# Decoder layer kernel: H chunks made earlier and in all quadrants, DVE and POOL kept off a shared port, W2's two parts in one product

## The chip, the cores and the metric

One core of a Trainium2 chip. The metric is the device time of one execution in microseconds, as the median of several runs; a lower time is better. The engines are called PE (TensorE), PEld (its weight loads), DVE (VectorE), ACT (ScalarE), POOL (GpSimd) and SP (SyncE, which here only issues DMAs).

## The reference

A decoder layer on `x` (4 x 512 rows of 256) with a second input of 4 x 64 context rows:

```
x = x + attn(layernorm(x))        # 16 heads of 16; softmax over the 4 rows of axis 0
x = x + xattn(layernorm(x), ctx)  # 16 heads of 64, per batch row of 512 queries, 64 keys
x = x + ffn(layernorm(x))         # 8 experts of 256 -> 1024 -> 256

def ffn(x):
    route_prob = softmax(xf @ Ws + bs).T              # (8, 2048)
    route_vals, routes = top_k(route_prob, 256)       # each expert takes its 256 best rows
    h = gelu(einsum('ekd,edf->ekf', xf[routes], W1) + b1)
    out = (einsum('ekf,efd->ekd', h, W2) + b2) * route_vals[..., None]
    return zeros.at[routes].add(out)
```

All is float32.

## The kernel before

One core does the whole layer. Every engine has one queue, written out by hand, and waits on semaphores. The rows are 16 tiles of 128 (`NT` = 16), four (`NJ`) per batch row; `D` = 256 is two chunks (`MC`) of 128.

**Precision.** A product whose operands are split into two fp32r parts is three matmuls (`product3`, L929 to L931): hi x hi, hi x lo, lo x hi. Other products are fp32 and show two records per matmul.

**Part 1** (to about 80 us) is the first attention, in four blocks of rows `j`, and among its steps the folded weights of the cross attention: `KV_product(c)` makes keys and values of chunk `c` (two of the 16 heads), `G_product(c)` multiplies the keys with the query weights. ACT evicts the high part of G (`G_evac`) and DVE the low part (`low_parts`). `mix_transpose(j)` needs POOL's sum `acc`, which needs DVE's `scale`; `y_product(j)` is followed by DVE's `add_residual(j)` and `statistics2(j)`, and POOL's inverse deviations. `turns` (L245 on) writes out by hand in which order each PSUM bank is used; `bank_free` and `bank_full` wait accordingly.

**Part 2** (to about 221 us) is the cross attention. `H` folds values and output weights: `pe_H` makes chunk `c` for the four batch rows (eight matmuls of 64 x 64 x 256 in two quadrants of the array), `act_H` evicts the high part, `dve_H` subtracts for the low part. The eight chunks are made in pairs ahead of the first four steps (`H_STEPS`, k = -3 to 0) of a software pipeline. A step `k` on PE (`pe_step`) is: the transposes of the probabilities of tile k, the transposes of the normalised rows of tile k+3 (`xn2`), the scores of tile k+2, the output product of tile k, and the logits of tile k-1. DVE (`dve_step`) takes the sums of tile k+1, the low parts of the probabilities (`PT_low`) and of `xT`, then the maximum (L1261) and the shifted scores (L1266) of tile k+2; ACT the exponential (L1097); POOL the division (L1137) and the additions to X. W1 and W2 of experts 0 to 3 are loaded and split (`W_high` on ACT, `W_low` on POOL) in the later steps; the last two halves are in the drain, the last of them after POOL's last normalised rows.

**Part 3** (about 221 to 248 us) finds each expert's 256th probability in 15 rounds (`SEARCHES`): DVE counts two trials (L1416, L1419), ACT one, PE adds over partitions, DVE takes the new floor. POOL meanwhile splits the probabilities into three bf16 parts (L1518 to L1522).

**Part 4** does the experts. For each one a list of its rows is made by DVE's one-hot (`onehot_of`, L1757) and 16 small matmuls (`list_of`, L1593), read by DVE (`read_list`), and used by POOL's indirect DMAs: a gather (L1698) of 256 rows and at the end a scatter-add (L1718). PE transposes the rows, makes the up product (8 x 2 x 3 matmuls of 256 columns) and the down product (2 x 8 x 3). ACT's GELU writes `hbuf`, two slots deep, and DVE makes `h_hi` (L1797) and `h_lo` (L1799); GELU of group n waits for `h_ready` n-1. `outputs(e)` scales and adds the result to `ybuf` (L1738). Ahead of expert 0, PE makes lists 0 and 1, seven unread matmuls (`UNREAD`, L1612), the transposes, and list 2; list 3 stands after the fourth of the up product's eight parts:

```
list_of(FIRST_LISTS[0])
list_of(FIRST_LISTS[1])
for _ in range(UNREAD): ...
transposes(EXPERTS[0])
list_of(FIRST_LISTS[2])
```

DVE reads lists 2 and 3 before it enters the loop over the experts.

Of the kernel before, what the change touches and what calls it, by code (L numbers as in the profile page):

```python
# [13 lines left out]
def build_program(nc, A, out):  # L14
# [11 lines left out]
    P = 128  # L26
# [93 lines left out]
    with ctx:  # L120
# [6 lines left out]
        def overlay(*sets):  # L127
# [5 lines left out]
            for k in order[:-1]:  # L133
# [11 lines left out]
        eps_col, warm = region([("eps_col", [P, 1], F32), ("warm", [P, 1], F32)])  # L145
# [31 lines left out]
        (H_hi, H_lo), attn, (W2_hi, W2_lo), (_, W2_raw) = overlay(  # L177
            [("H_hi", [P, CB, NC, D], F32R), ("H_lo", [P, CB, NC, D], F32R)],
            [("xn1", [P, T, D], F32), ("xnT", [P, MC, T, P], F32), ("q", [P, 2, T, D], F32),
             ("dif0", [P, NP, D], F32), ("sq", [P, NP, D], F32), ("acc", [P, T, D], F32),  # L180
             ("wqa", [P, MC, D], F32), ("dif1", [P, NP, D], F32),
             ("owT", [P, MC, D], F32), ("Nw", [P, MC, D], F32),
             ("MTs", [P, MC, P], F32), ("dist", [P, NP, HS], F32),
             ("Wk", [P, MC, HK], F32), ("bias_raw", [3 * NC, P], F32),
             ("b1_raw", [E * FC, P], F32), 
             ("outb_bc", [P, D], F32), ("Wq", [P, MC, HK], F32)],
            [("W2_hi", [P, 4, FC, D], F32R), ("W2_lo", [P, 4, FC, D], F32R)],
            [("beside2", [P, 4, FC, D], F32), ("W2_raw", [P, 4, FC, D], F32)])
        (xn1, xnT, q, dif0, sq, acc, wqa, dif1, owT, Nw, MTs, dist, Wk,
         bias_raw, b1_raw, outb_bc, Wq) = attn  # L190
# [65 lines left out]
        G_BANKS = (5, 5, 5, 2, 5, 2, 5, 2)  # L256
# [4 lines left out]
        def G_turns(c):  # L261
            return [(f"G{c}{m}", G_BANKS[c] + m, G_ready, MC * c + m + 1) for m in range(MC)]

# [8 lines left out]
        turns += KV_turns(3) + block_turns("M", 2) + G_turns(3) + KV_turns(4) + block_turns("y", 2) + G_turns(4)  # L272
        turns += KV_turns(5) + block_turns("M", 3) + G_turns(5) + KV_turns(6) + block_turns("y", 3)
        turns += KV_turns(7) + G_turns(6) + G_turns(7)
        part1 = len(turns)
        H_BANKS = ((4, 7), (5, 0), (1, 4), (7, 5), (4, 5), (7, 4), (5, 7), (4, 5))
        for c in range(NC):
            turns += [(f"H{c}{m}", H_BANKS[c][m], H_ready, 2 * c + m + 1) for m in range(2)]
# [594 lines left out]
        def sc(slot):  # L873
            return [banks[2 * slot], banks[2 * slot + 1]]
# [993 lines left out]
```

## Time and profile before

| | |
|---|---|
| median of 3 runs | 367.15 us (365.62 to 367.66) |
| the profiled execution | 367.29 us, span 365.5 us |
| PE busy | 321.0 us, 88% |
| DVE, ACT, POOL busy | 286.6, 189.5, 195.7 us |
| mean granted TensorE clock | 0.943 of full speed |

The span runs from the first to the last instruction; the execution's own time has some 1.8 us more. A busy PE is a PE with matmuls in flight: they are pipelined, so the duration of one is longer than the distance to the next. In the rows below times are us from the start of the span, mean durations ns.

### The profile page before, as it was taken

The page shows a single profiled execution, that of the slowest core. Times are in us where ns is not written, and L with a number is a line of the kernel's source. Part 1 is how long each engine was busy: PE and PEld are TensorE (multiplying, and loading weights), DVE is VectorE, ACT ScalarE, POOL GpSimd, SP SyncE. Part 2 cuts the span into 40 slices and gives each one's busy share as a digit, 9 for nine tenths or more (in the row PEclk, how much of TensorE's full clock was granted, in tenths as well). Part 3 has the DMA queues.
Part 4 walks back from the last instruction along what each step waited for, and adds up shares of the span by engine and source line. Part 5 has one row for each costly group of instructions (what it writes and reads, how often), then busy time and mean ns, then how long its engine had stood idle before and what let it go on. Part 6 is the DMA issues. An engine that isn't in the chain of part 4 may idle for free.

```text
span 365.5 us, 6473 instructions
## 1 busy us (share of the span) xinstructions
PE 321.0 (88%) x2350; PEld 290.6 (79%) x2350; DVE 286.6 (78%) x637; ACT 189.5 (52%) x374; POOL 195.7 (54%) x248
## 2 busy tenths in 40 slices
PE   7989998899979999999999991126999999999991
PEld 7877886675559999999999881116999999999991
DVE  3888888858777888888888778778578699689860
ACT  2677655446464457657764643682417546652230
POOL 3778789723042537888788764605224515543222
PEclk9999999999989999999999996555999999999997
DMA  8950000000000135143331537301158757611222
GB/s 251 382 208 1 2 0 2 0 0 3 0 2 0 38 121 165 39 145 97 105 130 57 159 103 230 116 1 43 45 165 240 184 204 190 173 20 40 30 30 29
DMA packets 24047, 34.29 MB, mean 94 GB/s; under 512 B 1784, under 2 KB 20560, under 8 KB 23888
## 3 DMA queue, kind: packets, MB, share of 16 engines
q1 hardware_dynamic: 20112, 29.36, 24.6%
q0 software_dynamic: 3072, 4.20, 6.5%
q10 hardware_dynamic: 832, 0.32, 0.4%
q8 instruction: 19, 0.31, 0.4%
q14 instruction: 12, 0.10, 0.1%
HBM read 27.58 MB, written 6.29 MB: 93 GB/s over the span
## 4 chain that ended last, share of the span: by engine, by line
PE 73%; DVE 13%; POOL 6%; ACT 4%; issue 2%; POOLq 0%; DVEq 0%; ACTq 0%
PE bank L929 13%; PE bank L931 13%; PE bank L930 13%; PE bank L939 4%; PE q_banks L929 4%; PE q_banks L930 4%; PE q_banks L931 4%; DVE flags_all L1419 2%; PE bank L1593 2%; PE bank L778 2%; PE q_banks L723 2%; PE bank L741 2%; PE bank L757 2%; POOL acc L410 1%; PE bank L957 1%
## 5 line engine op out<-in xcount | busy, mean ns | idle before, releaser
L1718 POOL DMA_INDIRECT out_x<-ybuf,idx x16 | 26.0, 1628 | 59.8 <-DVE ybuf L1738 57.7
L1137 POOL TENSOR_TENSOR prob<-prob,rsum 128x1024 f32<-128x1024 f32 x15 | 28.6, 1905 | 17.3 <-DVE rsum L1245 17.3
L929 PE MATMUL bank<-W_hi,h_hi 128*128 128x256 f32 x128 | 37.2, 291 | 0.0
L929 PE MATMUL bank<-H_hi,PT_hi 128*128 128x256 f32 x128 | 36.5, 285 | 0.1
L931 PE MATMUL bank<-H_hi,PT_lo 128*128 128x256 f32 x128 | 36.3, 283 | 0.0
L930 PE MATMUL bank<-H_lo,PT_hi 128*128 128x256 f32 x128 | 36.2, 283 | 0.0
L931 PE MATMUL bank<-W_hi,h_lo 128*128 128x256 f32 x128 | 36.2, 283 | 0.0
L930 PE MATMUL bank<-W_lo,h_hi 128*128 128x256 f32 x128 | 36.2, 283 | 0.0
L1097 ACT ACTIVATE prob<-prob 128x1024 f32<-128x1024 f32 x16 | 16.9, 1059 | 34.7 <-DVE prob L1266 34.7
L1675 ACT ACTIVATE hbuf<-bank,b_cols 128x256 f32<-128x256 f32 x32 | 13.4, 471 | 40.1 <-PE bank L931 40.1
L1698 POOL DMA_INDIRECT xg<-xn_rows,idx x16 | 18.7, 1168 | 20.7 <-DVE idx L1766 16.4
L1212 POOL TENSOR_TENSOR W_lo<-W_raw,W_hi 128x1024 fp32r<-128x1024 f32 x12 | 28.5, 2378 | 0.0
L929 PEld LDWEIGHTS bank<-H_hi,PT_hi 128*128 128x128 f32 x128 | 24.5, 192 | 0.7
L930 PEld LDWEIGHTS bank<-H_lo,PT_hi 128*128 128x128 f32 x128 | 24.5, 192 | 0.5
L929 PEld LDWEIGHTS bank<-W_hi,h_hi 128*128 128x128 f32 x128 | 24.7, 193 | 0.2 <-DVE h_lo L1799 0.2
L930 PEld LDWEIGHTS bank<-W_lo,h_hi 128*128 128x128 f32 x128 | 24.6, 192 | 0.0
L931 PEld LDWEIGHTS bank<-H_hi,PT_lo 128*128 128x128 f32 x128 | 24.5, 192 | 0.0
L931 PEld LDWEIGHTS bank<-W_hi,h_lo 128*128 128x128 f32 x128 | 24.5, 192 | 0.0
L1797 DVE CAST h_hi<-hbuf 128x512 fp32r<-128x512 f32 x32 | 13.7, 427 | 13.6 <-ACT hbuf L1675 13.5
L1799 DVE TENSOR_TENSOR h_lo<-hbuf,h_hi 128x512 fp32r<-128x512 f32 x32 | 22.2, 692 | 1.1
L1750 DVE TENSOR_TENSOR W_lo<-W_raw,W_hi 128x2048 fp32r<-128x2048 f32 x10 | 22.7, 2282 | 0.0
L1228 DVE TENSOR_TENSOR PT_lo<-bank,PT_hi 128x512 fp32r<-128x512 f32 x32 | 20.1, 667 | 1.3 <-ACT PT_hi L1055 1.1
(277 smaller groups left out, 1075.1 us busy)
## 6 DMA issues: line engine op xcount, KB each, us to landing
W_raw<-in_L_ffn_W SPq DMA_DIRECT2D x16, 1024.0 KB, 5.5
X<-in_x SPq DMA_DIRECT2D x4, 512.0 KB, 6.4
xn_rows<-xn SPq DMA_DIRECT2D x16, 128.0 KB, 1.7
out_x<-X SPq DMA_DIRECT2D x4, 512.0 KB, 3.7
Wq<-in_L_xattn_Wq SPq DMA_DIRECT2D x1, 1024.0 KB, 10.9
Wk<-in_L_xattn_Wk SPq DMA_DIRECT2D x1, 1024.0 KB, 13.8
Wv<-in_L_xattn_Wv SPq DMA_DIRECT2D x1, 1024.0 KB, 15.1
Wo<-in_L_xattn_Wo SPq DMA_DIRECT2D x1, 1024.0 KB, 17.1
```

Of the source, the lines that this page charges most:

```text
L929: t.matmul(out_ps, hi, rhs_hi, start=first, stop=False)
L930: t.matmul(out_ps, hi, rhs_lo, start=False, stop=False)
L931: return t.matmul(out_ps, lo, rhs_hi, start=False, stop=last_one)
L939: mm = t.transpose(banks[4 + g][:, c * P:(c + 1) * P], flat[:, o:o + P], ident[:])
L1097: a.activation(prob[:, s], prob[:, s], ACT.Exp).then_inc(exp_ready, 1)
L1137: g.tensor_tensor(prob[:, s], prob[:, s], rsum[:, s].unsqueeze(2).to_broadcast([P, HX, CK]), ALU.mult).then_inc(prob_ready, 1)
L1212: nc.gpsimd.tensor_tensor(lo[at], W[at], raw(hi[at]), ALU.subtract).then_inc(ready, 1)
L1228: nc.vector.tensor_tensor(PT_lo[:, n % 2, c], v3(banks[4 + g][:], 4), raw(PT_hi[:, n % 2, c]), ALU.subtract).then_inc(PT_ready, 1)
L1698: g.indirect_dma_start(xg[:, s, h], None, xn3_dram, bass.IndirectOffsetOnAxis(ap=idx[:, e, h:h + 1], axis=0), bounds_check=last_row, oob_i ...
L1718: g.indirect_dma_start(out_flat, bass.IndirectOffsetOnAxis(ap=idx[:, e, h:h + 1], axis=0), ybuf[:, h], None, bounds_check=last_row, oob_is ...
L1750: v.tensor_tensor(lo[at], W[at], raw(hi[at]), ALU.subtract).then_inc(late, 1)
L1799: v.tensor_tensor(h_lo[:, fs], hbuf[:, g_ % 2], raw(h_hi[:, fs]), ALU.subtract).then_inc(h_ready, 1)
```

## The change

- The region of H is laid out by chunk (chunk, part, batch row, column) over the buffers of part 1, those that die early first. W2 has the same order, so that the high and low part of one chunk and expert lie one step apart.
- Chunks 0 to 3 of H are made in part 1 (`EARLY_H`), among the later K, V and G; chunks 4 to 7 ahead of the steps k = -2, -1 and 0. DVE takes the low part of chunk 7 after the sums of step k = -1.
- `pe_H` sends odd batch rows to the other two quadrants, with the two heads of a chunk swapped; DVE writes the shifted scores of odd batch rows with heads swapped.
- The gate weights' subtraction goes from DVE to POOL. POOL's last `W_low` waits for the probabilities. The trials of the search are copied into PSUM and read there. DVE holds its second one-hot until POOL, by a small write (`asked`), has asked for expert 0's rows.
- Nine unread matmuls instead of seven; list 1 after the transposes of expert 0, lists 2 and 3 after the fourth and the eighth part of its up product.
- The down product of experts 0 to 6 multiplies `h_hi` with both parts of W2 in one matmul of 512 columns; DVE adds the second half of the bank in an instruction of its own, and waits for it. Expert 7 stays as before.

```diff
-        (H_hi, H_lo), attn, (W2_hi, W2_lo), (_, W2_raw) = overlay(
-            [("H_hi", [P, CB, NC, D], F32R), ("H_lo", [P, CB, NC, D], F32R)],
+        (H,), attn, (W2,), (W2_in,) = overlay(
+            [("H", [P, NC, 2, CB, D], F32R)],
...
-            [("W2_hi", [P, 4, FC, D], F32R), ("W2_lo", [P, 4, FC, D], F32R)],
+            [("W2", [P, FC, 2, 4, D], F32R)],
...
-        G_BANKS = (5, 5, 5, 2, 5, 2, 5, 2)
+        G_BANKS = (5, 5, 5, 5, 5, 5, 5, 2)
+        H_BANKS = ((2, 3), (2, 3), (2, 3), (2, 3), (4, 7), (5, 2), (4, 7), (4, 7))
...
             for j in range(NJ):
                 inverse_std(slice(j, NT, NJ), var2_ready, j + 1, rstd2_ready)
+            pool.wait_ge(cols_ready, 3)
+            g.tensor_tensor(ws_sb[:], ws_sb[:], gate_mean[:].unsqueeze(1).to_broadcast([P, MC, E]),
+                            ALU.subtract).then_inc(gate_ready, 1)
...
+            H_low = dve_H(dve)
             low_parts(2)
+            H_low(0)
             statistics2(0)
...
             add_residual(2)
             scale(3)
             low_parts(3)
-            dve.wait_ge(cols_ready, 3)
-            v.tensor_tensor(ws_sb[:], ws_sb[:], gate_mean[:].unsqueeze(1).to_broadcast([P, MC, E]),
-                            ALU.subtract).then_inc(gate_ready, 1)
+            H_low(1)
             statistics2(1)
             low_parts(4)
+            H_low(2)
             statistics2(2)
+            add_residual(3)
             low_parts(5)
-            add_residual(3)
+            H_low(3)
+            statistics2(3)
             low_parts(6)
-            statistics2(3)
             low_parts(7)
...
+            H_product = pe_H(pe)
             KV_product(3)
+            H_product(0)
             mix_transpose(2)
-            G_product(3)
             KV_product(4)
             y_product(2)
+            G_product(3)
+            H_product(1)
+            KV_product(5)
             G_product(4)
-            KV_product(5)
             mix_transpose(3)
-            G_product(5)
+            H_product(2)
             KV_product(6)
             y_product(3)
+            G_product(5)
+            H_product(3)
             KV_product(7)
...
-        H_BEFORE, H_BEFORE_ACT, H_BEFORE_EXP = ((0, 1), (2, 3), (4, 5), (6, 7)), ((0, 1), (2, 3), (5,), (7,)), {-2: 4, -1: 6}
+        H_BEFORE = ((), (4, 5), (6,), (7,))
+        H_BEFORE_ACT, H_BEFORE_EXP = ((), (4, 5), (), ()), {-2: 6, -1: 7}
+        H_BEFORE_LOW, H_AFTER_SUMS = ((), (4, 5), (6,), ()), {-1: 7}
...
-                for m in range(2):
-                    ps = bank_free(f"H{c}{m}")
-                    for b in (2 * m, 2 * m + 1):
-                        for rows in (slice(0, DK), slice(DK, P)):
-                            mm = t.matmul(ps[rows, (b % 2) * D:(b % 2 + 1) * D], V_T[rows, c, b], Wo[rows, c],
-                                          start=True, stop=True)
+                ps = [bank_free(f"H{c}{m}") for m in range(2)]
+                for b in range(CB):
+                    for h in range(2):
+                        rows, keys = head_rows(h), head_rows(h ^ b % 2)
+                        mm = t.matmul(ps[b % 2][keys, (b // 2) * D:(b // 2 + 1) * D], V_T[rows, c, b], Wo[rows, c],
+                                      start=True, stop=True)
...
+            pool.wait_ge(probs_ready, 1)
             W_low(pool, LAST_HALVES[1])
...
             if normed.within(NT):
                 v.reciprocal(rsum[:, normed.slot], sums[:, normed.slot]).then_inc(rsum_ready, 1)
+            if k in H_STEPS and k.n in H_AFTER_SUMS:
+                H_chunk(H_AFTER_SUMS[k.n])
...
+            trials = v3(banks[6][:, 0:4 * SEARCHES], SEARCHES)
+            order(v.tensor_copy(trials, trials_f[:]))
...
-                                                     in1=trials_f[:, r, b:b + 1].to_broadcast([P, P]), op0=ALU.subtract,
+                                                     in1=trials[:, r, b:b + 1].to_broadcast([P, P]), op0=ALU.subtract,
...
-        UNREAD = 7
+        UNREAD = 9
+        LISTS_AT = {FC // 2 - 1: 2, FC - 1: 3}
...
-                        if e == 0 and f == FC // 2 - 1:
-                            list_of(FIRST_LISTS[3])
+                        if e == 0 and f in LISTS_AT:
+                            list_of(FIRST_LISTS[LISTS_AT[f]])
...
+                            if e < E - 1:
+                                t.matmul(v3(banks[6 + h][:], 2), h_hi[:, f, hs], W2[:, f, :, p], start=f == 0, stop=False)
+                                mm = t.matmul(banks[6 + h][:, 0:D], h_lo[:, f, hs], W2_hi[:, p, f], start=False,
+                                              stop=f == FC - 1)
...
             gather(EXPERTS[0])
+            g.memset(asked[:], 0.0).then_inc(first_asked, 1)
...
+                    if e < E - 1:
+                        order(v.scalar_tensor_tensor(out=ybuf[:, h], in0=banks[6 + h][:, D:2 * D],
+                                                     scalar=gates[:, e, h:h + 1], in1=ybuf[:, h], op0=ALU.mult,
+                                                     op1=ALU.add))
...
             onehot_of(FIRST_LISTS[0])
+            read_list(FIRST_LISTS[0])
             split_vals_by_position(1)
-            read_list(FIRST_LISTS[0])
+            split_vals_beside_pool(2, E, order)
+            dve.wait_ge(first_asked, 1)
             onehot_of(FIRST_LISTS[1])
+            xgT_low(EXPERTS[0])
             read_list(FIRST_LISTS[1])
-            split_vals_beside_pool(2, E, order)
             onehot_of(FIRST_LISTS[2])
             onehot_of(FIRST_LISTS[3])
-            xgT_low(EXPERTS[0])
             read_list(FIRST_LISTS[2])
             read_list(FIRST_LISTS[3])
```

## Rows read from the trace of the kernel before

**Rows 1.** Stages: us, then busy us of each engine, clock, DMA.

```profile
core 0: us, PE busy (x) PEld busy (x) DVE busy (x) ACT busy (x) POOL busy (x), PEclk, DMA share, GB/s
60.00:80.60 20.60, 19.25 (x104) 15.37 (x103) 14.60 (x41) 8.26 (x18) 12.47 (x17) 1.00 0.00 1
...
105.35:108.77 3.42, 3.42 (x14) 3.13 (x15) 3.24 (x6) 1.95 (x4) 1.55 (x1) 0.50 0.00 0
...
297.30:310.30 13.00, 13.00 (x118) 12.96 (x117) 12.02 (x21) 7.63 (x13) 6.10 (x4) 1.00 0.73 203
```

**Rows 2.** Timeline of PE, 57 to 106 us: start, us, instruction, idle before.

```profile
57.65 1.09 PE L732 MATMUL bank<-ident,acc 128*128 128x128 f32 x8 [1.44 <-POOL acc L410]
...
69.52 1.09 PE L732 MATMUL bank<-ident,acc 128*128 128x128 f32 x8 [1.35 <-POOL acc L419]
...
80.64 3.67 PE L888 MATMUL bank<-Wo,V_T 64*64 64x256 f32 x32
85.07 0.41 PE L989 MATMUL bank<-ident,xn 128*128 128x128 f32 x2 [0.76 <-DVE G_lo L582]
...
96.41 0.44 PE L989 MATMUL bank<-ident,xn 128*128 128x128 f32 x2
...
102.93 1.08 PE L888 MATMUL bank<-Wo,V_T 64*64 64x256 f32 x8 [0.58 <-DVE H_lo L907]
105.28 1.89 PE L939 MATMUL bank<-ident,prob 128*128 128x128 f32 x8 [1.27 <-DVE H_lo L907]
```

**Rows 3.** Groups of instructions by line and form: busy us, mean ns.

```profile
L907 DVE TENSOR_TENSOR H_lo<-bank,H_hi 128x512 fp32r<-128x512 f32 x16 | 10.3, 683 | 2.3 <-ACT H_hi L899 2.1
...
L1738 DVE SCALAR_TENSOR_TENSOR ybuf<-bank,gates,ybuf 128x256 f32<-128x256 f32 x16 | 7.5, 483 | 3.8 <-PE bank L931 3.3
```

**Rows 4.** Timeline of DVE in the H stretch.

```profile
92.26 1.29 DVE L1261 TENSOR_REDUCE mx<-bank 128x8 f32<-128x512 f32 x2 [1.41 <-PE bank L931]
...
104.44 1.29 DVE L907 TENSOR_TENSOR H_lo<-bank,H_hi 128x512 fp32r<-128x512 f32 x2 [0.97 <-ACT H_hi L899]
```

**Rows 5.** Timeline of PE, fp32r products of 512 and of 256 columns.

```profile
109.41 0.40 PE L929 MATMUL bank<-G_hi,xT_hi 128*128 128x512 f32 x1
...
110.79 0.28 PE L929 MATMUL bank<-H_hi,PT_hi 128*128 128x256 f32 x1
...
113.18 0.28 PE L931 MATMUL bank<-H_hi,PT_lo 128*128 128x256 f32 x1
```

**Rows 6.** Timeline of DVE and POOL, 220 to 235 us.

```profile
220.81 0.23 DVE L1315 TENSOR_SCALAR probs<-logits,rowsum 128x8 f32<-128x8 f32 x1
222.02 2.44 DVE L1315 TENSOR_SCALAR probs<-logits,rowsum 128x8 f32<-128x8 f32 x1
222.09 2.34 POOL L1212 TENSOR_TENSOR W_lo<-W_raw,W_hi 128x1024 fp32r<-128x1024 f32 x1
...
232.59 0.35 DVE L1419 SCALAR_TENSOR_TENSOR flags_all<-high,floors,trials_f 128x128 bf16<-128x128 f32 x1
...
233.94 0.62 DVE L1419 SCALAR_TENSOR_TENSOR flags_all<-high,floors,trials_f 128x128 bf16<-128x128 f32 x1
```

**Rows 7.** Timeline of POOL and PE ahead of the first expert.

```profile
250.00 2.10 POOL L1698 DMA_INDIRECT xg<-xn_rows,idx  x1 [14.97 <-DVE idx L1766]
251.97 3.33 PE L1612 MATMUL q_banks<-ident 128*128 128x128 f32 x14
252.39 1.00 POOL L1698 DMA_INDIRECT xg<-xn_rows,idx  x1 [0.30 <-issue]
...
255.76 0.92 PE L1593 MATMUL bank<-vals_h,onehot 128*128 128x10 bf16 x13
...
256.86 0.39 PE L929 MATMUL bank<-xgT_hi,W_hi 128*128 128x256 f32 x1
```

**Rows 8.** Timeline of DVE and PE in the first expert.

```profile
261.03 0.16 DVE L1766 TENSOR_REDUCE idx<-bank 128x2 uint32<-128x4 f32 x1 [3.76 <-PE bank L1593]
...
263.43 0.43 DVE L1797 CAST h_hi<-hbuf 128x512 fp32r<-128x512 f32 x1
263.80 0.60 PE L1604 MATMUL bank<-ident,xg 128*128 128x128 f32 x4
263.89 0.69 DVE L1799 TENSOR_TENSOR h_lo<-hbuf,h_hi 128x512 fp32r<-128x512 f32 x1
```

**Rows 9.** Timeline of DVE after the first expert.

```profile
273.57 0.43 DVE L1797 CAST h_hi<-hbuf 128x512 fp32r<-128x512 f32 x1 [1.83 <-ACT hbuf L1675]
```

More of the change, by code:

```diff
@@ L262, in G_turns, with H_turns @@
             return [(f"G{c}{m}", G_BANKS[c] + m, G_ready, MC * c + m + 1) for m in range(MC)]
+        EARLY_H = 4
+        def H_turns(c):
+            return [(f"H{c}{m}", H_BANKS[c][m], H_ready, 2 * c + m + 1) for m in range(2)]
         def block_turns(what, j):
@@ L552, in act_part1 @@
             weights_of(3)
+            H_high = act_H(act)
             KV_evac(3)
+            H_high(0)
             mixT_evac(2)
+            KV_evac(4)
             G_evac(3)
-            KV_evac(4)
+            H_high(1)
+            KV_evac(5)
             G_evac(4)
-            KV_evac(5)
             mixT_evac(3)
+            H_high(2)
+            KV_evac(6)
             G_evac(5)
-            KV_evac(6)
+            H_high(3)
             KV_evac(7)
@@ L861, in build_program, with run_steps @@
         H_STEPS = STEPS[:LEAD_T + 1]
-        H_BEFORE, H_BEFORE_ACT, H_BEFORE_EXP = ((0, 1), (2, 3), (4, 5), (6, 7)), ((0, 1), (2, 3), (5,), (7,)), {-2: 4, -1: 6}
-        def run_steps(step, H_chunk=None, H_before=H_BEFORE):
+        H_BEFORE = ((), (4, 5), (6,), (7,))
+        H_BEFORE_ACT, H_BEFORE_EXP = ((), (4, 5), (), ()), {-2: 6, -1: 7}
+        H_BEFORE_LOW, H_AFTER_SUMS = ((), (4, 5), (6,), ()), {-1: 7}
+        def run_steps(step, H_chunk, H_before=H_BEFORE, before=lambda nth: None):
             for nth, k in enumerate(STEPS):
-                for c in H_before[nth] if H_chunk and k in H_STEPS else ():
-                    H_chunk(c)
+                if k in H_STEPS:
+                    before(nth)
+                    for c in H_before[nth]:
+                        H_chunk(c)
                 step(k)
@@ L898, in H_chunk @@
                     ps = bank_full(act, f"H{c}{m}")
-                    a.activation(H_hi[:, 2 * m:2 * m + 2, c], v3(ps[:], 2), ACT.Copy).then_inc(H_hi_ready, 1)
+                    a.activation(H_hi[:, m::2, c], v3(ps[:], 2), ACT.Copy).then_inc(H_hi_ready, 1)
             return H_chunk
@@ L1229, in PT_low, with dve_step @@
                                         ALU.subtract).then_inc(PT_ready, 1)
-        def dve_step(dve, k, order):
+        def dve_step(dve, k, order, H_chunk):
             v = nc.vector
@@ L1265, in dve_step @@
                     dve.wait_ge(max_ready, 2 * n + g + 1)
-                    ins = v.tensor_tensor(prob[:, s, hs], ps, mx[:, s, hs].unsqueeze(2).to_broadcast([P, 8, CK]),
-                                          ALU.subtract)
+                    pairs = lambda ap: ap.rearrange("p (a h) k -> p a h k", h=2)
+                    shifted_to = pairs(prob[:, s, hs])
+                    if new.group % 2:
+                        shifted_to = shifted_to[:, :, ::-1]
+                    ins = v.tensor_tensor(shifted_to, pairs(ps),
+                                          pairs(mx[:, s, hs].unsqueeze(2).to_broadcast([P, 8, CK])), ALU.subtract)
                 ins.then_inc(shifted, 1)
@@ L1367, in pool_part2 @@
             pool.wait_ge(ld["small"], 32)
-            run_steps(lambda k: pool_step(pool, k, order))
+            for k in STEPS:
+                pool_step(pool, k, order)
             pool_drain(pool, order)
```

76 lines of the change are left out of this document (38 added, 38 removed).

## The prediction

> **What bounds the kernel now.** I read the page first, then the table of stages, then the timelines of the places that the diff touches. In the stage table the reader is to see that PE is busy 19.25 of 20.60 us ahead of the H stretch, that in the H stretch its clock was once at half (1.2 GHz, for 3.42 us), and that in the third expert's period PE is busy throughout and DVE 12.02 of 13.00 us beside it [rows 1]. So a saving counts only if it is in PE's own work, or in one of the places where PE waits: ahead of the mix transposes, between the last G and the first scores, in the search, and at the first expert.
>
> **The H chunks.** Before, H costs PE 3.67 us for two chunks (32 records, with their tail), some 1.75 us each [rows 2]: eight fp32 products of 256 columns that run two by two. With the other two quadrants beside them I take half, 0.9 us with tail; the bound above is the old 1.75 (nothing gained), the one below the 0.86 of a clean half. The Trainium skill (TensorE: Matmul & The Clock Gate, Measured speedup vs the span model) has tiles of the array run side by side, more of them giving more; no row here shows four. By it the chunk would cost 0.86 us.
>
> Chunk 0 goes into the 1.44 us in which PE waits for POOL at 57.65, chunk 1 mostly into the 1.35 us at 69.52 [rows 2]. PE's other work between the two is the same in another order, and before it was through at 68.2 (69.52 less the wait); with chunk 1 it is at 69.1, where POOL's sum is just ready (its inputs, y 2 and the scaling, come 0.6 us earlier). Chunks 2 and 3 then cost 1.8, so the last G ends at 82.0 instead of 80.6. ACT's parts follow about 1 us behind. DVE has the eight low parts of four chunks more, 8 x 0.683 = 5.5 us [rows 3], and loses the gate subtraction, which POOL now does behind its last inverse deviation (by about 84.8; queued behind it are only POOL's additions to X, and PE waits for it ahead of all of this stretch's work). DVE was busy 14.60 of 20.60 us here [rows 1], so it now closes the stage: the low parts of G 5 and H 3, the statistics (1.8) and the low parts of G 6 and 7 (two of 0.68 us each) follow one another from 78.3 to 85.0. The first row transpose then starts at 85.3, against 85.07 before [rows 2]. Bounds: 84.2 (DVE keeps up with PE) and 86.9 (chunks at 1.75).
>
> Then only chunks 4 and 5 stand ahead of the first scores: these end at 90.7 instead of 92.26. The third row transpose waits for DVE's maximum and shift, ACT's exponential and the normalised rows queued behind it; that chain, from 92.26 to 96.41 before, is unchanged, 4.2 us: 94.95 [rows 2, 4]. The second scores (12 products of 0.23) end at 98.05. Now the price. Chunk 7 is made on PE after them (99.0), ACT's part ends at 99.9, and DVE has its low part in its queue ahead of xT_lo, the maximum and the shift of row block 1, which all wait: shift 1 ends at 103.5, the exponential at 104.5, the fourth transpose is at 105.2. Before, PE came to it only at 107, since the probability transposes waited until 105.28 for the low part of the last chunk, on DVE from 104.44 [rows 2, 4]. Scores 2 (12 x 0.23) and the first output (24 x 0.1195) [rows 5] bring PE to its second probability transposes at 111.1, against 113.8 (the output's first product at 110.79 and 24 more): -2.7 us, if the clock stays.
>
> It won't. Before, PE was idle 0.58 and 1.27 us in the last microseconds before 105.35 and then ran at half clock for 3.42 us, fully busy [rows 1, 2]: 1.7 us lost. The change empties PE more: idle 3.2 us ahead of 85.3, 3.3 ahead of 94.95, 5.2 of the 6.2 ahead of 105.2. Each is longer than the two gaps that were followed by the fall; the single wait of 1.44 us at 57.65 was not followed by one. What a fall costs is 0 to 1.7 us, by where it lies on the work. I take 1.7 for the last and half, 0.85, for each of the first two: 3.4 us, so this stretch ends 0.7 us later than before. Bounds: -2.7 (no fall) and +2.4 (three full ones). The Trainium skill (TensorE: Matmul & The Clock Gate, What's actually happening) says that idleness brings the array to the slow clock and sustained work takes it back; it speaks against emptying PE, and the row agrees. By it all three gaps are followed by a fall.
>
> **The steady steps** (to 205.4) are bound by PE's own products; the shift with heads swapped writes as many elements, in the same instruction form. Nothing, bounds 0 and +0.3.
>
> **The port.** At 222.02 DVE's last scaling of the probabilities takes 2.44 us instead of 0.23 (the same form at 220.81): POOL's W_lo, from 222.09 to 224.43, stands beside it [rows 6]. It is on the path: PE's transpose and the search follow. With POOL waiting for it, 2.2 us are saved. The copy of the trials into a bank (60 elements, and a wait for it) mostly hides behind PE's transpose: +0.1; bounds 0 and 0.3. W_lo now runs beside the start of the search, where no DVE instruction reads two tensors from SBUF. The search rounds that stand beside POOL's splitting of the values have counts of up to 0.62 us where they take 0.35 [rows 6], some 0.5 in all; with the trials in PSUM they should not, but the key combination, two SBUF inputs, moves into the same window: -0.35; bounds -0.5 and 0. Sum -2.45, bounds -2.7 and 0 (if W_lo blocks the next instructions instead). The Trainium skill (SBUF — State Buffer, Who interferes with whom) says that a DVE instruction with at most one SBUF input outside the two-port modes doesn't meet POOL; the rows agree. By it -2.4 stands.
>
> **The first expert.** POOL's first gather took 2.10 us beside DVE's one-hot, the second 1.00 [rows 7]. With the one-hot held until POOL has asked, both take 1.00: rows land 1.1 us earlier, PE's nine unread products (18 records of 0.22 us, from 249.5; before 14 from 251.97) end at 253.5, and the up product starts 1.2 us earlier. But list 2 was in the shade of the gathered rows' split (from 255.76, ahead of the up product at 256.86) and now stands between up products: +1.0 us. And list 3 moves from the middle of the up product to its end, while DVE's read of it stays ahead of the first h_hi. Before, DVE waited 3.76 us for it, to 261.03, then began its groups (0.43 and 0.69 us each, 1.06 with their overlap), had the fourth at 266, and PE's transposes at 263.80 and the down product behind them were hardly held [rows 8]. After, list 3 ends at 263.6 (search shift left out), the first cast starts at 263.9 and, with two hbuf slots making GELU wait for DVE, the four groups are ready at 265.0, 266.0, 267.2 and 268.3. PE's first half of the down product ends at 269.05 instead of 267.0: +2.0. With -0.14 of the product below: 1.65 us later in all. Bounds: 0.8 (groups at 1.0 us, no GELU wait) and 3.35 (PE's idle 2.0 us there brings one more fall of the clock).
>
> **W2's parts in one product.** Two of 256 columns cost 2 x 0.1195, one of 512 0.23 [rows 5]: 9 ns, x16 per expert, 0.14 us, for six more experts -0.8; bounds 0 and -1.2 (rounding of the 0.23). DVE adds two of 0.483 us [rows 3] and two waits, 1.1 us per expert. After the first expert it had 1.83 us idle [rows 9]: hidden. After three of the others (the third among them, 12.02 of 13.00 us [rows 1]) it had next to none; it arrives 1.5 us late at the next cast, and PE has 1.3 to 1.4 us of room before the last group: +0.3 in all, bounds 0 and 2. Without that room it would cost 1.1 per such expert, 3.3.
>
> **Sum.** +0.7 - 2.45 + 1.65 - 0.8 + 0.3 = -0.6. The profiled execution took 367.29 us (span 365.5 and 1.8 around it), so 366.7; against the median of 367.15, 366.5. About 0.5% (1.8 us) is what a measurement can tell from no change, so this is "no change". Within this case: 365.3 to 368.0.
>
> **Rivals.**
> PE keeps its clock in the H stretch. For it: gaps of 1.4 us did nothing. Against: the row at 105.35. With one fall, -1.0 in place of +0.7: 364.8; with none 363.1. Chance 0.27.
> The clock falls wherever PE waits, with full price: three falls in H (+2.4) and one in the first expert's down product (+1.7). That is 369.9; it decides, from +1.85 over the median, once at least 2.4 of these 3.4 us come. For it: 2 us of idle within 5 us there. Chance 0.17. By the Trainium skill (TensorE: Matmul & The Clock Gate, What's actually happening), which lets the slow clock follow idleness, this is the case to expect.
> The four quadrants do not run side by side: chunks stay at 1.75, the first transpose comes 1.6 us later, 368.1. Against: the pairs do. Chance 0.09.
> The port isn't freed, the search's start waits as the scaling did: 2.35 us back, 368.9. Chance 0.07.
> My case: 0.40.
>
> **How the numbers follow.** Faster by over 0.5% (under 365.3): the first rival and a tail of my own case, 0.32. Slower (over 369.0): the second rival, half of the last two and a tail, 0.24. Within: 0.44. The range takes the first rival down to 363.3 and the second up to 369.3.
>
> **What would show it.** The line of H for two chunks near 1.8 us in place of 3.67; first transpose near 85.3; second probability transposes between 111 and 116, with granted clock 0.5 in one to three stretches between 82 and 110; DVE idle before the low part of chunk 7; the scaling at 0.23 us; the first gather at 1.0 us; DVE waiting some 6 us for list 3 and PE waiting for h_lo at the first expert; a period of 12.8 us after. I am wrong if H's stretch ends far from 114.5, or if GELU and DVE overlap so that PE doesn't wait there.

## The result

The changed kernel takes 373.0 us (median of 4 runs, 370.6 to 373.7) against 366.4 for the kernel before on the same chip: 1.0154 times the time, 95% interval 1.012 to 1.0188. It is slower by 5.6 us going by the ratio (6.6 by the two medians), above the range of the prediction. The profiled execution took 372.68 us, with a span of 370.9 against 365.5. Times of one and the same kernel, the one before included, come in groups some 2 us apart: over all its runs the kernel before took 365.3 to 366.0 or 366.9 to 368.5 us.

The table of stages of the changed kernel, at the places where the clock fell in the profiled execution, between the stretch ahead of them and the third expert; it answers to [rows 1]:

```profile
core 0: us, PE busy (x) PEld busy (x) DVE busy (x) ACT busy (x) POOL busy (x), PEclk, DMA share, GB/s
60.00:80.60 20.60, 20.60 (x140) 15.19 (x140) 18.08 (x48) 10.10 (x21) 12.40 (x17) 1.00 0.00 1
84.38:91.21 6.83, 5.64 (x39) 3.29 (x40) 2.85 (x6) 3.37 (x8) 1.60 (x4) 0.50 0.01 2
98.04:101.45 3.41, 3.41 (x10) 2.68 (x9) 0.70 (x2) 0.38 (x1) 2.59 (x2) 0.50 0.00 0
108.28:115.10 6.82, 5.14 (x13) 4.13 (x14) 2.99 (x6) 3.27 (x6) 2.60 (x2) 0.50 0.01 2
258.46:261.88 3.42, 3.42 (x19) 3.42 (x18) 2.22 (x2) 0.84 (x2) 2.80 (x2) 0.51 0.13 38
297.00:310.00 13.00, 13.00 (x102) 12.15 (x101) 12.76 (x21) 7.63 (x15) 3.73 (x4) 1.00 0.71 192
```

Where [rows 1] has one stretch at half clock (3.42 us), there are now four, outside the search and the end. In the three of the H stretch PE was busy for 5.64 + 3.41 + 5.14 = 14.2 us; the same work takes half of that at full clock, so 7.1 us went there, against 1.7 before (an estimate from these rows; the runs below bear it out).

PE's timeline of the changed kernel through the H stretch, to be laid beside [rows 2]:

```profile
64.82 1.09 PE L915 MATMUL q_banks<-Wo,V_T 64*64 64x256 f32 x16
65.84 1.13 PE L771 MATMUL bank<-ctxT,Wk 128*128 128x256 f32 x4
...
68.86 1.09 PE L746 MATMUL bank<-ident,acc 128*128 128x128 f32 x8
...
81.26 1.03 PE L784 MATMUL q_banks<-kT,WqT 64*128 64x256 f32 x8
85.57 0.66 PE L1017 MATMUL bank<-ident,xn 128*128 128x128 f32 x2 [3.28 <-DVE G_lo L594]
...
97.78 0.46 PE L1017 MATMUL bank<-ident,xn 128*128 128x128 f32 x2 [3.13 <-ACT xn L1388]
...
102.49 1.09 PE L915 MATMUL bank<-Wo,V_T 64*64 64x256 f32 x16
105.16 1.06 PE L967 MATMUL bank<-ident,prob 128*128 128x128 f32 x8 [1.57 <-DVE H L935]
109.96 0.69 PE L1017 MATMUL bank<-ident,xn 128*128 128x128 f32 x2 [3.74 <-ACT xn L1388]
...
118.25 1.04 PE L967 MATMUL bank<-ident,prob 128*128 128x128 f32 x8
```

The waits are where they were expected (3.28, 3.13, 1.57 and 3.74 us), the first row transpose too (85.57), and a chunk takes 1.02 us from start to start. But the second probability transposes stand at 118.25, where before they stood at 113.67: 4.6 us.

The rest, from two timelines of the changed kernel, DVE and POOL first, against [rows 6, 7]:

```profile
226.88 0.23 DVE L1350 TENSOR_SCALAR probs<-logits,rowsum 128x8 f32<-128x8 f32 x1
...
236.32 0.35 DVE L1455 SCALAR_TENSOR_TENSOR flags_all<-high,floors,bank 128x128 bf16<-128x128 f32 x1
...
237.46 0.48 DVE L1471 SCALAR_TENSOR_TENSOR keys<-high,thr,low 128x128 f32<-128x128 f32 x1
...
252.10 1.33 POOL L1740 DMA_INDIRECT xg<-xn_rows,idx  x1 [12.54 <-DVE idx L1813]
...
267.63 0.16 DVE L1813 TENSOR_REDUCE idx<-bank 128x2 uint32<-128x4 f32 x1 [3.74 <-PE bank L1631]
```

and PE at the first expert, against [rows 7, 8]:

```profile
256.62 0.33 PE L1642 MATMUL bank<-ident,xg 128*128 128x128 f32 x1 [0.93 <-DMA xg<-xn_rows,idx]
...
257.99 0.39 PE L957 MATMUL bank<-xgT_hi,W_hi 128*128 128x256 f32 x1
...
262.46 1.16 PE L1631 MATMUL bank<-vals_h,onehot 128*128 128x10 bf16 x16
...
266.44 1.16 PE L1631 MATMUL bank<-vals_h,onehot 128*128 128x10 bf16 x16
...
269.07 0.47 PE L1687 MATMUL bank<-W,h_hi 128*128 128x512 f32 x1 [0.98 <-DVE h_lo L1847]
```

The differences of the two timelines add up to the whole: +4.6 in the H stretch; +0.3 in the steady steps (7.35 us each, 7.32 before; the twelve score products take 2.84 us instead of 2.82, some 2 ns more each, why is open); -2.8 from there to the end of the search, since the scaling is back at 0.23 us and the counts at 0.35; +3.7 to expert 1's up product (276.89, before 271.06); -0.5 over the seven experts after. Before rounding the sum is +5.4, as the spans.

### The profile page after: what moved, and what is told of

It reads as the page before. It is cut to its first block, busy times and chain, and to the rows that moved or that the text cites. A ratio compares the mean times of both kernels' runs of the same rounds, so it can differ in the third digit from the quotient of the medians.

```text
span 370.9 us, 6275 instructions
## 1 busy us (share of the span) xinstructions
PE 321.9 (87%) x2242; PEld 284.5 (77%) x2242; DVE 288.8 (78%) x651; ACT 188.9 (51%) x374; POOL 195.9 (53%) x250
## 4 chain that ended last, share of the span: by engine, by line
PE 74%; DVE 13%; POOL 6%; ACT 3%; issue 2%; DMA 1%; POOLq 0%; ACTq 0%; DVEq 0%
PE bank L957 9%; PE bank L958 9%; PE bank L959 9%; PE bank L1687 7%; PE q_banks L957 4%; PE q_banks L958 4%; PE q_banks L959 4%; PE bank L967 3%; PE bank L1688 3%; DVE flags_all L1455 2%; PE bank L1631 2%; PE bank L792 2%; PE bank L771 2%; PE q_banks L737 2%; PE bank L755 2%
## 5 line engine op out<-in xcount | busy, mean ns | idle before, releaser
L1687 PE MATMUL bank<-W,h_hi 128*128 128x512 f32 x112 | 41.4, 410 | 1.2 <-DVE h_lo L1847 1.0
L957 PE MATMUL bank<-H,PT_hi 128*128 128x256 f32 x128 | 36.5, 285 | 0.1
L959 PE MATMUL bank<-H,PT_lo 128*128 128x256 f32 x128 | 36.3, 283 | 0.0
L958 PE MATMUL bank<-H,PT_hi 128*128 128x256 f32 x128 | 36.3, 283 | 0.0
L1688 PE MATMUL bank<-W,h_lo 128*128 128x256 f32 x112 | 31.5, 281 | 0.0
L1687 PEld LDWEIGHTS bank<-W,h_hi 128*128 128x128 f32 x112 | 21.2, 190 | 7.0 <-issue 1.2
L957 PEld LDWEIGHTS bank<-H,PT_hi 128*128 128x128 f32 x128 | 24.5, 192 | 0.7
L958 PEld LDWEIGHTS bank<-H,PT_hi 128*128 128x128 f32 x128 | 24.5, 192 | 0.5
L959 PEld LDWEIGHTS bank<-H,PT_lo 128*128 128x128 f32 x128 | 24.5, 192 | 0.0
L1688 PEld LDWEIGHTS bank<-W,h_lo 128*128 128x128 f32 x112 | 21.2, 190 | 0.0
L1717 ACT ACTIVATE hbuf<-q_banks,b_cols 128x256 f32<-128x256 f32 x32 | 13.4, 471 | 14.2 <-DVE h_lo L1847 8.5
L1268 DVE TENSOR_REDUCE sums<-prob 128x16 f32<-128x1024 f32 x15 | 18.3, 1220 | 2.0 <-ACT prob L1125 1.5
L957 PE MATMUL bank<-xgT_hi,W_hi 128*128 128x256 f32 x64 | 19.0, 296 | 0.0
```

The source lines that it names most:

```text
L957: t.matmul(out_ps, hi, rhs_hi, start=first, stop=False)
L958: t.matmul(out_ps, hi, rhs_lo, start=False, stop=False)
L959: return t.matmul(out_ps, lo, rhs_hi, start=False, stop=last_one)
L1268: last = v.tensor_reduce(sums[:, normed.slot], prob[:, normed.slot], AX.X, ALU.add)
L1687: t.matmul(v3(banks[6 + h][:], 2), h_hi[:, f, hs], W2[:, f, :, p], start=f == 0, stop=False)
L1688: mm = t.matmul(banks[6 + h][:, 0:D], h_lo[:, f, hs], W2_hi[:, p, f], start=False, stop=f == FC - 1)
```

## The experiments

The ratios are against the kernel before, run beside each experiment on the same chip; its median moved between 366.0 and 367.6 us from one such set to the next. So a difference under some 2 us between medians of different sets says little, and small terms are read from traces, by milestones.

**Is it the clock?** The first kernel puts unread products into PE's waits in the H stretch of the changed one:

```diff
+            if k.n == -3:
+                unread(bank_free("H40"), 13)
+            if k.n == -1:
+                pe.wait_ge(H_ready, max(H_last[2:4]))
+                unread(banks[2], 13)
+            if k.n == 0:
+                pe.wait_ge(shifted, 1)
+                unread(banks[0], 8)
...
                     prob_transposes(n, g)
+                if k.n == 0:
+                    unread(banks[0], 12)
```

> The changed kernel, with unread 128x128 products on PE in its waits of the H stretch: 13 ahead of the first row transpose, 13 after chunk 6, 8 after chunk 7 and 12 behind the first probability transposes. Theory A (the half clock follows PE's idle time, and it is what the stretch costs): no half clock between 82 and 115 us; the scores end at 90.7, the third row transpose stands at 95, the second probability transposes at 111.5 in place of 118.25, and the kernel takes 366.3 us in place of 373.0. Theory B (the waits for DVE and ACT themselves are the price, the clock only goes with them): the milestones stay within 1 us of the changed kernel's and the time is 372.5 to 374.

Measured: 368.8 us (1.0058, 1.0025 to 1.0092). No half clock between 82 and 115, but 2.5 us over the 366.3 expected. The profiled execution, near the median, was 2.4 us late at the end of the last G: 0.9 of it since the first full clock came at 8.0 us instead of 5.9, the rest by a half clock near 21 us. And the first 13 stood behind PE's wait for the gate weights, which POOL has only at 86.9 in that trace, so they pushed the first row transpose back by another 2.1 us. The second kernel has them ahead of that wait:

```diff
         def pe_part2(pe):
+            unread(bank_free("H40"), 13)
             pe.wait_ge(ones_ready, 1)
```

> As the first filled kernel, but the 13 unread products of the first wait stand ahead of PE's wait for the gate weights, so that they run from 82.3 us while POOL and DVE finish, instead of behind it. Theory A (idle time brings the half clock, and the half clock is the H stretch's loss): no half clock from 82 to 115, the first row transpose at 85.7, the second probability transposes at 111.3 to 111.8 and 366.5 us, 2 us below the first filled kernel. Theory B (the stretch is set by its chain of waits, and the clock isn't the cost): within 1 us of the first filled kernel or slower.

Measured: 365.8 us (0.9972, 0.9949 to 0.9996), 7 us below the changed kernel. Its profiled execution was its slowest (368.1): it too was 2.4 us late at the last G, with a first full clock at 8.0 us and a half clock near 21 us, and it has one more half clock at the first expert, from 253.7 to 257.1 us. Less the 2.4, the second probability transposes stand at 111.5, as expected. One row of its stage table, one of the changed kernel's:

```profile
84.00:116.00 32.00, 31.09 (x256) 26.06 (x253) 22.45 (x42) 15.43 (x32) 8.51 (x11) 1.00 0.01 2
```

```profile
82.00:115.00 33.00, 21.27 (x119) 14.44 (x116) 18.18 (x34) 12.87 (x27) 8.48 (x11) 0.74 0.00 1
```

Nothing but useless work and two waits for it were added, and 7 us went. Theory A holds, theory B is out. One wait alone (13, 0, 0, 0):

> The changed kernel with 13 unread products in the first of its waits alone (82.3 to 85.5). Theory A (each wait brings its own fall): the half clock at 84.4 to 91.2 goes, those after 98 and 108 stay, the third row transpose stands at 95 and the second probability transposes 2.6 us earlier than 118.25: 370.4 us. Theory B (the fall is only put off to the next wait at a longer price): 372.5 us or more.

Measured: 369.4 us (1.0056, 1.0028 to 1.0084), 3.6 less than the changed kernel where 2.6 was expected. Its profiled execution was the slowest by far, 374.2 us, and the ratio leaves it out: late by 2.3 us like the two traces above, and at half clock after the search to 263.8 us and again from 270.6. Only its H stretch is read here: the probability transposes stand at 117.93, so 2.6 earlier when the 2.3 are taken off. Of its trace, the row of the wait that is filled and that of the two that are not:

```profile
84.00:95.00 11.00, 10.16 (x96) 7.37 (x92) 8.13 (x18) 6.50 (x16) 3.32 (x7) 1.00 0.01 2
96.00:111.00 15.00, 8.31 (x40) 5.90 (x41) 7.14 (x12) 4.67 (x9) 2.59 (x2) 0.75 0.00 1
```

The falls behind the two waits that were not filled stay, so they don't hang on the first. But such a wait isn't followed by a fall each time. The kernel with `UNREAD = 13` and the earlier lists (below) has the H stretch of the changed kernel, and in its profiled execution (365.6 us) the clock stays full behind the same wait of 3.28 us and falls only at 94.3 (3.4 us long) and 104.6 (6.8):

```profile
85.44 0.41 PE L1017 MATMUL bank<-ident,xn 128*128 128x128 f32 x2 [3.28 <-DVE G_lo L594]
...
95.01 0.69 PE L1017 MATMUL bank<-ident,xn 128*128 128x128 f32 x2 [3.13 <-ACT xn L1388]
```

Without the first fall its third row transpose comes at 95.01 instead of 97.78: 2.8 us, half of the 5.64 us that PE was busy in that fall.

**Quadrants alone.** The kernel before, with `pe_H` and the swapped shift of the changed one, its eight chunks left in place:

> The kernel before, with H in four quadrants and the shifted scores with heads swapped, all eight chunks where they were. Theory A (less work in a stretch of waits turns into idle time, and idle time into half clock): two chunks take 1.9 us in place of 3.67, PE waits 2.5 us ahead of the first row transpose and 1 to 3 us ahead of the later ones; the second probability transposes come 1.5 us earlier if the clock falls once and later than 113.8 if it falls twice: 365 to 368 us, spread over runs. Theory B (PE's own work sets the stretch): 3.5 us less or more, 362.5 us.

Measured: 370.9 us (1.0107, 1.0073 to 1.0141): PE's work fell by some 6 to 7 us (an estimate: four pairs of chunks, the first 3.67 to 1.96, the second to 2.29) and the kernel became 4 us slower, more than theory A had asked. PE's timeline:

```profile
84.73 0.41 PE L991 MATMUL bank<-ident,xn 128*128 128x128 f32 x2 [2.48 <-DVE G_lo L582]
...
94.41 1.99 PE L889 MATMUL bank<-Wo,V_T 64*64 64x256 f32 x16 [2.24 <-DVE H_lo L909]
...
103.38 1.09 PE L889 MATMUL bank<-Wo,V_T 64*64 64x256 f32 x16 [2.24 <-DVE H_lo L909]
106.04 1.94 PE L941 MATMUL bank<-ident,prob 128*128 128x128 f32 x8 [1.56 <-DVE H_lo L909]
```

There is no fall behind the first of these waits. The rows behind the second and the fourth show the half clock by their length: 1.99 us for 16 records that take 1.09 behind the third, 1.94 for eight transposes that take 1.03 at full clock. The same kernel with 10, 9, 9 and 6 unread products in its waits:

> The kernel before with H in four quadrants, as the earlier run of 370.9 us, and with unread products in PE's four waits there (10, 9, 9 and 6). Theory A (the quadrants alone lost time because they turned work into idle time and so into half clock): no half clock from 80 to 115, the second probability transposes at 112.3 to 113.3, 364.5 us. Theory B (the swapped heads or the new bank order cost it): 370 us or more.

Measured: 367.4 us (0.9996, 0.9972 to 1.002). No half clock in the stretch and the transposes at 112.70, as asked, so theory A holds for the stretch and theory B is out; but the time is 3 us above what was asked. The profiled execution (368.4 us) has the full clock back only at 259.9 us, inside the up product of expert 0, where the kernel before has it at 255.5. So, too, with the kernel before itself (3, 1, 2 and 5 products):

> The kernel before with 3, 1, 2 and 5 unread products in its four waits of the H stretch, nothing else. Theory A: its one fall at 105.35 goes, 1.5 us less than before. Theory B (waits of 0.4 to 1.3 us don't bring it; something else does): the fall stays and the time is the same or up to 0.5 us more.

Measured: 367.1 us (0.9984, 0.9961 to 1.0007). The fall is gone, the transposes come at 112.13, the search starts 1.5 us earlier, and it is all given back. Rows of its stage table and, below, of the kernel before:

```profile
80.00:115.00 35.00, 35.00 (x253) 25.09 (x250) 28.95 (x56) 20.93 (x41) 8.35 (x10) 1.00 0.00 1
256.00:259.07 3.07, 3.07 (x16) 3.07 (x16) 0.00 (x0) 0.75 (x2) 1.97 (x2) 0.52 0.20 53
```

```profile
80.00:115.00 35.00, 31.95 (x225) 22.72 (x222) 27.55 (x52) 19.44 (x38) 8.33 (x10) 0.95 0.00 1
256.00:259.07 3.07, 3.07 (x32) 2.99 (x32) 1.15 (x5) 1.09 (x4) 1.30 (x3) 1.00 0.15 43
```

With 16 records where there were 32, the up product of expert 0 now runs at half clock: the full clock, back at 255.5 before, comes back at 259.0. The up product starts at 255.35, 1.5 us earlier than before, and list 3, behind half of it, stands at 259.92, where it stood at 259.83. Two kernels tried to mend that with unread products between lists 0 and 1:

```diff
             list_of(FIRST_LISTS[0])
+            for _ in range(6):
+                t.matmul(banks[2][:, 0:P], ident[:], ident[:], start=True, stop=True)
             list_of(FIRST_LISTS[1])
```

> The kernel before with its waits in the H stretch filled (as in the run of 367.1 us) and with 6 unread products more between lists 0 and 1, in PE's wait of 1.46 us. Theory A (the gain of 1.5 us in the H stretch was given back since the full clock came back only after 259 us, in the up product): the clock is full from 256 us at the latest and the time is 365.4 us in most runs. Theory B (the gain is lost elsewhere, whatever the clock does there): 367 us again.

Measured: 367.0 us (1.0006, 0.9985 to 1.0026). The clock is full from 254.9 in its trace, but the six took 2.91 us in a wait of 1.46 and moved list 1 by 1.1 us. Three in their place:

> The kernel before with its H stretch filled and 3 unread products (1.3 us at half clock) in PE's wait between lists 0 and 1. Theory A: list 1 is where it was, full clock by 256 us, 365.5 us. Theory B: 367 us as with six or with none.

Measured: 367.3 us (0.9996, 0.9973 to 1.002): 4 of 12 runs at 365.3 to 365.8, the profiled one among them (full clock from 253.5), 8 at 367.0 to 368.2. That the late return ate the gain is shown for the one execution traced with none. That three products prevent it in most runs isn't shown, nor, with one trace each, that the edit moved the return.

**The first expert.** 13 unread products ahead of it (`UNREAD = 13`):

> The changed kernel with 13 unread products in place of 9 ahead of expert 0's transposes, so that PE no longer waits 0.93 us for the second half of the gathered rows. Theory A: the half clock at 258.5 to 261.9 goes, and with it 1.5 us in the first up product: 371.5 us. Theory B (that fall has nothing to do with PE's idle time): 373.0 to 373.3 us, with the first transposes 0.9 us later.

Measured: 371.0 us (1.0103, 1.0068 to 1.0139), 2.0 less; no half clock in its up product. The lists earlier (`LISTS_AT = {1: 2, FC // 2 - 1: 3}`):

> The changed kernel with list 2 after the second and list 3 after the fourth part of expert 0's up product, in place of the fourth and the eighth. Theory A (DVE's read of list 3 ahead of its first h_hi holds PE at the down product): DVE starts h_hi some 4 us earlier, PE's wait of 0.98 us and its stops between the groups go, 2.2 us less: 370.8 us. Theory B (GELU's two slots hold PE there, whenever DVE begins): under 0.7 us less.

Measured: 372.5 us, but its 12 runs lie in two lots, four from 366.4 to 370.9 us and eight from 372.2 to 373.0, and the ratio (1.0076, 1.0035 to 1.0118) is of the four. The 370.8 that theory A asked can't be judged by that. PE no longer waits for `h_lo`, but the profiled execution (372.7) has the half clock from 258.9 for 10.2 us, all through the up product, so it says little. Hence both together, the H stretch as changed:

> The changed kernel with 13 unread products and with the lists after the second and fourth part of the up product; the H stretch as changed. It stands beside the kernel with the 13 products alone (371.0 us), both with PE kept at full clock in expert 0. Theory A (DVE's late read of list 3 costs 2.2 us): 368.8 us, PE without a wait between expert 0's up and down product. Theory B (that wait comes back later): 370.5 us or more.

Measured: 368.5 us (1.0008, 0.9979 to 1.0038), but again in two lots, five of 12 runs from 365.4 to 365.6 and seven from 367.6 to 369.4. So the 2.5 us by the medians can be in part clock in the H stretch, where its trace above lacks a fall. At the first expert both profiled executions are at full clock, and there the lists can be read, from expert 0's up product to expert 1's, first with the 13 alone, then with both:

```profile
258.16 0.39 PE L957 MATMUL bank<-xgT_hi,W_hi 128*128 128x256 f32 x1
...
275.59 0.28 PE L957 MATMUL bank<-xgT_hi,W_hi 128*128 128x256 f32 x1
```

```profile
254.72 0.38 PE L957 MATMUL bank<-xgT_hi,W_hi 128*128 128x256 f32 x1
...
270.01 0.28 PE L957 MATMUL bank<-xgT_hi,W_hi 128*128 128x256 f32 x1
```

17.43 us against 15.29: 2.1 us, as theory A had it.

**The port**, on the kernel before (POOL's wait, and the trials from PSUM):

> The kernel before, with the port's two edits alone (POOL's last low part of W2 waits for the probabilities; the trials are read from PSUM). My theory: the last scaling takes 0.23 us and the counts beside POOL 0.35 us, so 2.5 to 2.7 us less, 363.8 us beside 366.4. Rival (the low part only blocks the search's first instructions instead): 366 us or more.

Measured: 364.5 us (0.9928, 0.9901 to 0.9955): 2.6 us less by the ratio; the scaling at 0.23 us in its trace.

**W2**, in the changed kernel (the two conditions `e < E - 1` never true):

> The changed kernel with all experts' down products in three matmuls of 256 columns, as before, and without DVE's second additions. My theory (the 512-column product saves 0.14 us per expert and DVE's additions cost 0.3 us in all): 0.5 us more, 373.5 us. Rival (DVE's additions are what the experts' period now waits for): 1 us or more less.

Measured: 373.1 us (1.0152, 1.0105 to 1.0199), 369.6 to 374.5: nothing can be read from the time at this spread. The traces can: from expert 0's up product to expert 7's it is 93.94 us, and 93.28 in the changed kernel.

**All mends**: the filled H stretch, `UNREAD = 13` and the earlier lists.

> The changed kernel with the H stretch filled as in the kernel beside it, 13 unread products ahead of expert 0 and the lists earlier. If the three losses (H stretch 6.5 us, the fall in the first up product 1.5 to 2, DVE late for list 3 2.2) are independent: 362.5 us, below both kernels. If the time between them is shared, 364 to 366.

Measured: 362.75 us (0.9886, 0.9858 to 0.9914), its six runs within 1 us. Below both kernels, and 0.25 from what independent losses would give. PE's timeline, at full clock from 6 to 221 us:

```profile
85.38 0.41 PE L1029 MATMUL bank<-ident,xn 128*128 128x128 f32 x2
...
94.96 0.44 PE L1029 MATMUL bank<-ident,xn 128*128 128x128 f32 x2
...
105.55 0.44 PE L1029 MATMUL bank<-ident,xn 128*128 128x128 f32 x2 [0.84 <-ACT xn L1401]
...
111.45 1.03 PE L967 MATMUL bank<-ident,prob 128*128 128x128 f32 x8
```

From here single terms can be read. W2's parts in two products again:

> The kernel with all mends (362.75 us), with the down products in three matmuls of 256 columns and without DVE's second additions. My theory (0.14 us per expert saved, against 0.3 us of DVE): 0.5 us more, 363.2 us. Rival (the 512-column product saves only the 5 ns by which it is shorter, or DVE's additions cost more): 362.6 us or less.

Measured: 363.2 us (0.99, 0.9868 to 0.9931), 0.46 more by the medians. The two ratios' intervals overlap over most of their width, and this profiled execution was 0.7 us late already at the last G, with its first full clock at 7.4 us instead of 6.1, so the medians don't decide. From expert 0's up product to expert 7's the traces have 90.35 us against 89.67, that is 0.68 more, some 0.1 per expert: the rival is out. The port as before:

> The kernel with all mends, but the port as before: POOL's last low part doesn't wait for the probabilities, the trials are read from SBUF. My theory (the scaling of 2.44 us and the counts beside POOL): 2.5 us more, 365.2 us. Rival (the time is made up by the unread products ahead of expert 0): under 1 us more.

Measured: 365.3 us (0.9951, 0.9931 to 0.9971), 2.6 more (2.4 by the ratios). The two rows have come back together:

```profile
220.23 2.44 DVE L1361 TENSOR_SCALAR probs<-logits,rowsum 128x8 f32<-128x8 f32 x1
220.30 2.34 POOL L1252 TENSOR_TENSOR W<-W_in,W 128x1024 fp32r<-128x1024 f32 x1
```

The lists as in the changed kernel:

> The kernel with all mends, but lists 2 and 3 after the fourth and eighth part as in the changed kernel. Theory A (DVE's read of list 3 holds the down product): 2.2 us more, 364.9 us. Theory B (part of it is idle time that is lost anyway): 1 us more or less.

Measured: 364.8 us (0.9951, 0.9927 to 0.9976), 2.1 more, with PE's wait back:

```profile
260.46 0.47 PE L1700 MATMUL bank<-W,h_hi 128*128 128x512 f32 x1 [0.98 <-DVE h_lo L1860]
```

Its profiled execution also has a half clock of 3.4 us in the down product behind that wait; how much of the 2.1 is clock in the median run isn't known, but the two traces at full clock above gave 2.1 without any.

**What is left in the H stretch at full clock.** All mends, and DVE's low part of chunk 7 behind the shift of row block 1:

```diff
-        H_BEFORE_LOW, H_AFTER_SUMS = ((), (4, 5), (6,), ()), {-1: 7}
+        H_BEFORE_LOW, H_AFTER_SUMS = ((), (4, 5), (6,), (7,)), {}
```

> The kernel with all mends (362.75 us), with DVE's low part of chunk 7 behind the maximum and shift of row block 1 instead of ahead of them, and one unread product in place of 12 behind the first probability transposes. Theory A (the low part in the queue is what delays the fourth row transpose at full clock): DVE's shift ends near 100.5 in place of 103.9, the fourth row transpose stands at 103, the second probability transposes 2.5 us earlier, 360.3 us. Theory B (a later link, the low parts of the probabilities or the exponential, holds the step then): under 0.7 us less.

Measured: 359.7 us (0.9796, 0.9764 to 0.9829), 359.0 to 359.9: the best, 2% below the kernel before. Timelines of DVE and of PE:

```profile
98.05 1.29 DVE L1304 TENSOR_REDUCE mx<-q_banks 128x8 f32<-128x512 f32 x2 [1.92 <-PE q_banks L959]
99.26 1.28 DVE L1313 TENSOR_TENSOR prob<-q_banks,mx 128x512 f32<-128x512 f32 x2
100.45 1.28 DVE L935 TENSOR_TENSOR H<-bank,H 128x512 fp32r<-128x512 f32 x2
```

```profile
102.41 0.38 PE L1029 MATMUL bank<-ident,xn 128*128 128x128 f32 x2
108.23 1.03 PE L967 MATMUL bank<-ident,prob 128*128 128x128 f32 x8
```

The fourth row transpose comes at 102.41 instead of 105.55, the probability transposes 3.2 us earlier: the whole gain. The low part now stands in DVE's time while ACT takes the exponential, where only PE's first probability transposes wait for it, 0.26 us.

## Why the prediction was wrong

**The step that failed** is the price of the clock in "The H chunks": "What a fall costs is 0 to 1.7 us, by where it lies on the work", taken as 3.4 us for three falls, 5.1 at most. That price came from the one fall of [rows 1], 3.42 us long. The changed kernel had the three falls in the places named, but two of them lasted 6.83 us, with PE busy for 5.64 and 5.14 of it, and the third 3.41, all busy: 7.1 us. The unread products show the same from the other side: at full clock the stretch ends at 111.45, with the falls at 118.25, 6.8 us later. A fourth fall is missing from the sum: 3.4 us in expert 0's up product. A bound and the second rival had one in the down product, behind PE's wait for `h_lo`; it came instead behind a wait of 0.93 us for the gathered rows, which the prediction didn't have, and costs 1.5 us in the trace, 2.0 by the run without it. Add these two errors, 3.7 and 1.5, to the forecast of -0.6 and it is +4.6, against +5.4 in the spans.

**The rivals.** "The clock falls wherever PE waits" comes nearest, with 0.17: right in the H stretch, in the wrong place at the first expert, and too low at 369.9 for the same mis-sized price. The first rival (the clock is kept) is out for this kernel: it argued from gaps of 1.4 us, while the new ones are 3.1 to 3.7. But one of them, of 3.28 us, was passed at full clock in the trace with both first-expert edits, so how many falls there are is in part luck of the execution. Quadrants and port did what they should. The Trainium skill (TensorE: Matmul & The Clock Gate, What's actually happening) made falls at all three gaps the case to expect, as I read it. The changed kernel's trace agrees, that other trace agrees for two of three. I gave it the lower chance, since the row at 57.65 had shown a wait without a fall.

**Right, term by term.** First row transpose 85.3, found 85.57 (85.38 with all mends). Third 94.95, found 94.96 at full clock; fourth 105.2, found 105.55; second probability transposes 111.1, found 111.45. So the chain of waits was right to 0.4 us, and only what the clock made of it was not. A chunk: 0.9, found 1.02. The port and the search: -2.45; -2.8 in the trace, 2.6 by the medians of each of the two runs. First gather 1.0: 1.33, still partly beside DVE; the up product's earlier start -1.2: -0.97. List 2 +1.0: 1.02. DVE late for list 3 +2.0: 2.2 in the trace (1.27 at the start of the down product, 0.94 between its groups), 2.1 by the run and by the two traces at full clock. W2 and its additions -0.5: -0.66 and -0.68 in two pairs of traces. Steady steps 0: +0.3. Two signs were not met: the experts' period was to be 12.8 us and is 12.95 (13.05 before), close to what the prediction's own saving of 0.14 us gives, and DVE's wait for list 3 was to be some 6 us and is 3.74, behind one of 2.98 for list 2.

**What the prediction did not see.** The kernel before seems to pay such prices in a changing number of places: its runs of 365.3 to 366.0 us have a mean granted clock of 0.947 to 0.951, those of 366.9 to 368.5 at most 0.944. No run of the first lot was traced, so the places aren't known. The first full clock comes 4.9 to 8.0 us after the start in the traces, and what follows moves with it. And a gain in one place can be given back where the clock returns: a saving of some 7 us of PE's work (quadrants alone) cost 4 us, and with its waits filled it gained nothing.

**Open**: why the score products of the changed kernel are longer by some 2 ns; why a wait of the same length is followed by a fall in one execution and not in another; what decides in which runs the kernel before keeps its clock at the first expert.

## What to carry to other kernels

Work taken off an engine that then waits for others was worth nothing by itself here, and on TensorE it cost: behind new waits of 3.1 to 3.7 us the clock was at half for 3.4 or 6.8 us, with one such wait seen without. Before thinning out PE's work in a stretch bound by a chain through other engines, shorten the chain, or keep PE busy with unread products that end before the real work is due, and count the falls in the trace. Read small terms between two milestones of traces at the same clock: so 0.7 us and 2.1 us could be told, where the same edits drowned in times that spread over 4 to 7 us.

## What was unexpected in the hardware

Useless matmuls made the kernel 7 us faster (373.0 to 365.8). The half clock lasted 3.4, 6.8 or 10.2 us, though PE was busy for most of it (5.64 of 6.83 us, and all of the 10.2), and in kernels with the same code up to that place it came in some executions and not in others: the one near 21 us in three of the traces, the one from 84.3 to 84.8 us on in four of the five that have a wait of 3.1 to 3.3 us there. The Trainium skill (TensorE: Matmul & The Clock Gate, What's actually happening) says that the moment of a change is not tied to the kernel's own start and varies from run to run; the groups of times agree with that, but no run here shows the cause. And in the trace of a kernel that was earlier by 1.5 us the full clock came back at 259.0 instead of 255.5 us, which ate the 1.5 us.
